# Row maxima of a streaming context attention: two of thirteen key ranges maximised as one pair, b + relu(a - b)

## Chip, cores and metric

The kernel runs on one core of one Trainium2 chip. The time is device microseconds of one execution; the profile's span runs from the first to the last instruction of one profiled execution. The engines are named as in the profile: PE is TensorE (PEld its weight loads), DVE is VectorE, ACT is ScalarE, POOL is GpSimd and SP is SyncE. They run side by side, each through its own instructions in order, and wait for each other by semaphores.

## What is computed

A decoder of two layers over 1024 tokens of width 128. Layer 0 is a Mamba block, an attention to a context of 6404 rows, and a mixture of experts; layer 1 is an attention over the tokens, a second attention to the context, and another mixture of experts. Each branch is added to its input and layer-normalised. The change is in layer 0's attention to the context, where 16 heads of width 8 share one set of keys and values:

```
c = concat([mem, kv], axis=1)             # the context rows; here only ctx_1024, 6404 of them
qh = (q @ w_q) as 16 heads of width 8
kvp = c @ w_kv
k, v = kvp[..., :8], kvp[..., 8:]
attn_prob = softmax(qh @ k.T / sqrt(8))   # 16 heads x 1024 queries x 6404 keys
out = (attn_prob @ v) as 128 columns @ w_concat
```

The softmax is taken with the row's maximum subtracted, so every query and head needs the maximum over its 6404 scores before any exponential of its row can be taken.

## The kernel before

Queries are worked through in 16 blocks. A block is 128 tokens by 8 heads, 1024 query rows. Two things are done for every block.

**Maxima.** For each of the 8 heads, 13 score tiles of 128 queries by 512 keys (the last one 260 wide) are made by PE (`max_tile`, L836) into a PSUM ring of four banks, `max_ps`. DVE takes the maximum of each tile along its keys into one column of `max_partial` (`maximum`, L1069): 104 reductions for a block. After each half of a block (`"A"` is heads 0 to 3, `"B"` heads 4 to 7) DVE reduces the columns, negates the result and splits it into a high and a low part (`negate`, L1080 to L1082), PE turns these (L843), and ACT copies them into the stacked queries (`take_shift`, L861). The maximum is thus subtracted inside the score matmul.

**Exponentials.** A block's scores come a second time, now with keys on the partitions: 51 chunks of 128 keys, each in two halves of 512 query rows, 102 steps that the code calls `e`. At step `e` PE makes the score tile (`score`, L974) into one of three banks and ACT takes its exponential into `probs` (`exponentiate`, L1053), which holds three chunks. PE multiplies the probabilities by the values (`weigh`, L963), with the sums of the probabilities in an extra column. Step `e` waits until the exponential of step `e - 3` is done. `weigh` stands behind every third step: one chunk behind steps with `e % 6 == 5`, two chunks behind steps with `e % 6 == 2`.

**The order.** While block b is exponentiated, the maxima of block b + 1 are made. A list written out in advance (`items_at`) says which maximum tile follows which score on PE: 103 tiles over the first 100 steps, about one behind each score. A maximum tile may be issued when the tile four places earlier in that list has been read (`free_place`). The two matmuls of a step stand on different halves of PE's rows. Block 0's maxima are made ahead of all exponentials, between other matmuls (queries, values, and the keys and values of layer 1).

**Keys.** They are made earlier, beside the Mamba block: `ContextKeys.make` (L365) multiplies a range of 512 context columns by the key weights, repeated over the rows; ACT adds a constant (`high_on_act`), and DVE subtracts half of the rows (`halve`, L377). The last ranges are made at the end of the Mamba block, where PE's next work is Mamba's output matmuls (L598).

## Time and profile before

| | us |
|---|---|
| median of 3 runs | 2043.5 |
| lowest and highest run | 2041.26, 2043.7 |
| profiled execution: span | 2039.6 |
| profiled execution: its own time, beside the span | not listed apart; the median is 3.9 above the span |
| PE busy | 1959.2 (96%) |
| DVE busy | 1573.2 (77%) |
| ACT busy | 1355.8 (66%) |
| POOL busy | 100.9 (5%) |

The page gives each engine's busy time and its share of the span. PE's ends are modelled and its matmuls overlap, so 96% does not say that PE is at its peak. The granted clock of PE was 0.986 of full speed over the span, and 1.00 through the whole of the attention that is changed, from 200 to 1250 us.

### The profile page before, as it was taken

To read this page: it belongs to the slowest core of one execution; us is meant where nothing else is said; L and a number is where in the kernel's file an instruction comes from. 1 tells how busy PE (TensorE), PEld (TensorE's weight loads), DVE (VectorE), ACT (ScalarE), POOL (GpSimd) and SP (SyncE) were. 2 spreads that over 40 slices of the span, in tenths; PEclk is the share of its full clock that TensorE was granted. 3 is DMA by queue.
4 is the path that set the end of the run, shared out by engine and by line. 5 is a ranking of instruction groups with operands and counts; after the bars stand their busy time and mean duration, and the time that the engine had idled before them with its cause. 6 is when DMAs were issued, how large, how long until landed. Compare 5 with 4: busy or idle time off the path is not lost. (4 is left out here: it accounts for less than half of the span.)

```text
span 2039.6 us, 36001 instructions
## 1 busy us (share of the span) xinstructions
PE 1959.2 (96%) x14245; PEld 969.3 (48%) x14245; DVE 1573.2 (77%) x2868; ACT 1355.8 (66%) x2394; POOL 100.9 (5%) x85
## 2 busy tenths in 40 slices
PE   7779999999999999999999999999999998999997
PEld 2225744444444444444444444444344444777755
DVE  7997899999999999999999981233688865444344
ACT  5333488888888888888888887432578874443321
POOL 1661000000000000000000000000200000000000
PEclk8999999999999999999999999999999999999999
DMA  4210000000000000000000000232000000000000
GB/s 148 73 62 0 1 2 2 2 1 2 1 1 2 2 1 2 2 2 1 1 2 1 2 2 1 60 120 65 0 1 1 2 1 0 1 1 1 16 29 28
DMA packets 25043, 32.66 MB, mean 16 GB/s; under 512 B 5967, under 2 KB 20335, under 8 KB 24622
## 3 DMA queue, kind: packets, MB, share of 16 engines
q1 hardware_dynamic: 23694, 28.30, 4.5%
q8 instruction: 111, 1.82, 0.4%
q10 hardware_dynamic: 1184, 2.10, 0.3%
q14 instruction: 54, 0.44, 0.1%
HBM read 29.61 MB, written 0.65 MB: 15 GB/s over the span
## 5 line engine op out<-in xcount | busy, mean ns | idle before, releaser
L1069 DVE TENSOR_REDUCE sb_max_partial<-ps_max_ps 128x1 f32<-128x512 f32 (+1 forms) x1664 | 977.3, 662 | 43.9 <-PE ps_max_ps L836 43.1
L1053 ACT ACTIVATE sb_probs<-ps_score_ps 128x512 f32<-128x512 f32 (+1 forms) x1632 | 875.1, 597 | 117.6 <-PE ps_score_ps L974 71.7
L974 PE MATMUL ps_score_ps<-sb_q_stack,sb_key_stack 64*128 64x512 f32 x1632 | 586.6, 443 | 3.9 <-ACT sb_probs L1053 3.4
L836 PE MATMUL ps_max_ps<-sb_key_stack,sb_q_stack 64*128 64x512 f32 (+1 forms) x1560 | 555.9, 438 | 0.0
L963 PE MATMUL ps_acc_ps<-sb_probs,sb_val_ones 128*32 128x256 f32 x6528 | 465.0, 387 | 0.0
L974 PEld LDWEIGHTS ps_score_ps<-sb_q_stack,sb_key_stack 64*128 64x128 f32 x1632 | 275.8, 183 | 321.5 <-ACT sb_probs L1053 257.2
L836 PEld LDWEIGHTS ps_max_ps<-sb_key_stack,sb_q_stack 64*128 64x128 f32 x1560 | 265.0, 184 | 9.8 <-DVE sb_max_partial L1069 7.5
L963 PEld LDWEIGHTS ps_acc_ps<-sb_probs,sb_val_ones 128*32 128x32 f32 x6528 | 156.3, 108 | 207.7 <-issue 140.5
L1721 DVE TENSOR_REDUCE sb_s_max_partial<-ps_s_ps 128x1 f32<-128x512 f32 x256 | 158.5, 682 | 24.6 <-PE ps_s_ps L1567 24.5
L1708 ACT ACTIVATE sb_s_probs<-ps_s_ps 128x512 f32<-128x512 f32 x256 | 140.8, 597 | 30.8 <-PE ps_s_ps L1595 22.8
L1942 DVE TENSOR_SCALAR_CACHE_REDUCE sb_x_scores<-ps_x_score_ps 128x1024 f32<-128x1024 f32 (+1 forms) x56 | 62.0, 1110 | 69.2 <-PE ps_x_score_ps L1929 69.2
L1977 ACT COPY sb_x_turned<-ps_x_turn_ps 128x512 f32<-128x512 f32 (+1 forms) x52 | 29.5, 568 | 116.8 <-PE ps_x_turn_ps L1967 116.8
L1987 PE MATMUL ps_x_acc_ps<-sb_x_turned,sb_val 128*128 128x256 f32 (+1 forms) x408 | 105.4, 381 | 0.0
L1567 PE MATMUL ps_s_ps<-sb_s_key_stack,sb_s_q_stack 64*128 64x512 f32 x256 | 103.5, 462 | 1.9 <-DVE sb_s_q_stack L1521 1.5
L1595 PE MATMUL ps_s_ps<-sb_s_q_stack,sb_s_key_stack 64*128 64x512 f32 x256 | 103.4, 464 | 0.3 <-ACT sb_s_q_stack L1699 0.2
L1929 PE MATMUL ps_x_score_ps<-sb_key_T,sb_x_q_T 128*128 128x512 f32 (+1 forms) x208 | 97.7, 579 | 1.8 <-DVE sb_x_scores L1942 1.8
L1300 DVE TENSOR_TENSOR sb_e_hidden<-sb_e_hidden,sb_e_gate_rows 128x1024 f32<-128x1024 f32 x30 | 36.7, 1226 | 75.6 <-ACT sb_e_hidden L1292 60.3
L471 PE MATMUL ps_mamba_ps<-sb_xpad,sb_ident 128*128 128x512 f32 x128 | 65.2, 632 | 23.0 <-POOL sb_xpad L536 23.0
L640 ACT ACTIVATE sb_val<-sb_delta,sb_a_neg 128x1024 f32<-128x1024 f32 x32 | 36.6, 1148 | 74.0 <-DVE sb_key_T L697 69.3
L1292 ACT ACTIVATE sb_e_hidden<-ps_e_hid_ps,sb_e_b 128x1024 f32<-128x1024 f32 x34 | 37.9, 1113 | 71.4 <-PE ps_e_hid_ps L1268 71.4
L1606 PE MATMUL ps_s_ps<-sb_s_probs,sb_s_val_ones 128*32 128x256 f32 x1024 | 81.8, 391 | 0.2 <-ACT sb_s_probs L1708 0.2
L536 POOL TENSOR_TENSOR sb_xpad<-sb_key_T,sb_val 128x1024 f32<-128x1024 f32 x31 | 73.9, 2383 | 58.3 <-DVE sb_key_T L697 57.2
(299 smaller groups left out, 1802.7 us busy)
## 6 DMA issues: line engine op xcount, KB each, us to landing
sb_val<-c_rows SPq DMA_DIRECT2D x16, 512.0 KB, 3.6
sb_e_gate_rows<-e_gate_dram SPq DMA_DIRECT2D x15, 512.0 KB, 3.9
...
```

The lines of the kernel that those rows point to most:

```text
L836: nc.tensor.matmul(bank((blk, u))[:, 0:n], queries, keys, start=True, stop=True).then_inc(tile_ready, 1)
L963: ins = nc.tensor.matmul(acc_ps[32 * q:32 * q + 32, 0:QUART], k.val_ones[:, v, :], probs[:, v % 3, q * QUART:(q + 1) * QUART], start=(v == ...
L974: nc.tensor.matmul(score_ps[:, e % 3, :], k.key_stack[rows(blk), c * P:(c + 1) * P], q_stack[rows(blk), blk // 2, j * HALF:(j + 1) * HALF] ...
L1053: nc.scalar.activation(probs[0:n, c % 3, j * HALF:(j + 1) * HALF], score_ps[0:n, e % 3, :], ACT.Exp).then_inc(exp_done, 1)
L1069: nc.vector.tensor_reduce(partial[:, blk % 2, h, r:r + 1], bank((blk, u))[:, 0:RANGES[r][1]], AX.X, ALU.max).then_inc(tile_used, 1)
L1567: nc.tensor.matmul(bank((blk, u)), q_stack[rows(blk), blk // 2, t * P:(t + 1) * P], key_stack[rows(blk), blk // 2, r * HALF:(r + 1) * HALF ...
L1595: nc.tensor.matmul(score_ps[:, n % 3, :], key_stack[rows(blk), blk // 2, c * P:(c + 1) * P], q_stack[rows(blk), blk // 2, j * HALF:(j + 1) ...
L1606: ins = nc.tensor.matmul(acc_ps[32 * q:32 * q + 32, 0:QUART], val[:, v, head(blk), :], probs[:, n % BUFS, q * QUART:(q + 1) * QUART], star ...
L1708: nc.scalar.activation(probs[:, n // 2 % BUFS, (e % 2) * HALF:(e % 2 + 1) * HALF], score_ps[:, n % 3, :], ACT.Exp).then_inc(exp_done, 1)
L1721: nc.vector.tensor_reduce(partial[:, blk % 2, t, r:r + 1], bank((blk, u)), AX.X, ALU.max).then_inc(tile_used, 1)
L1929: ins = nc.tensor.matmul(score_ps[:, at % 2, (i % 2) * HALF:(i % 2) * HALF + n], q_T[:, t * P:(t + 1) * P], k.key1_T[:, i * HALF:i * HALF ...
L1987: ins = nc.tensor.matmul(acc_ps[:, p % 2, 0:2 * P], k.val1[0:keys, c, :], turned[0:keys, G % DEPTH, 2 * j * P:2 * (j + 1) * P], start=(c = ...
```

## The change

For every head of every block, the score tile of range 7 is no longer made. In its place PE makes the tile of a difference: queries times (keys of range 7 minus keys of range 11). Call the scores of range 7 a and those of range 11 b. ACT takes relu(a - b) of that tile into an SBUF tile `raised` (`raise_tile`, L1106 of the changed kernel). When the tile of range 11 comes, DVE adds `raised` to it and takes the maximum of the sum in one call (`tensor_tensor_reduce`, L1117). As b + relu(a - b) is max(a, b), the one column stands for both ranges, and `max_partial` has 12 columns for a head in place of 13.

The difference of the keys is a 14th range of `key_stack`, made like the others: two matmuls into one bank, the first with the key weights on the columns of range 7, the second with their negative (`wk_neg`, made by POOL) on those of range 11. It is made last, after range 12. To make room in SBUF, two other tiles now share memory with older ones (`res` of the first norm with `delta`, `fin_merged` with `wk_rep`).

```
+RAISED, PLAIN_OF_PAIR = 7, 11
+DIFF_AT = NCH * P
...
-    BANK = (4, 5, 6, 7, 0, 2, 3, 0, 0, 1, 0, 1, 0)
+    BANK = (4, 5, 6, 7, 0, 2, 3, 0, 0, 1, 0, 1, 0, 1)
-    AFTER = {7: 5, 10: 9, 11: 10, 12: 11}
+    AFTER = {7: 5, 10: 9, 11: 10, 12: 11, 13: 12}
...
+        if r == self.DIFF:
+            pe.wait_ge(self.k_done, self.AFTER[r])
+            (a0, n), (b0, _) = self.RANGES[RAISED], self.RANGES[PLAIN_OF_PAIR]
+            nc.tensor.matmul(self.bank(r), k.wk_rep[:], k.ctx_T[:, a0:a0 + n], start=True, stop=False)
+            nc.tensor.matmul(self.bank(r), k.wk_neg[:], k.ctx_T[:, b0:b0 + n], start=False, stop=True).then_inc(self.k_made, 1)
+            return
...
+        for j in range(2 * 4):
+            lo = j // 4 * (P // 2) + j % 4 * HD
+            ins = nc.gpsimd.tensor_scalar(k.wk_neg[:, lo:lo + HD], w_kv[:, 0:HD], -1.0, None, ALU.mult)
...
             def max_tile(pe, blk, u):
-                h, (c0, n) = u // NR, RANGES[u % NR]
+                h, (c0, n) = u // NR, RANGES[u % NR] if u % NR != RAISED else (DIFF_AT, HALF)
...
                         nc.scalar.activation(probs[0:n, c % 3, j * HALF:(j + 1) * HALF], score_ps[0:n, e % 3, :],
                                              ACT.Exp).then_inc(exp_done, 1)
+                        for b, u in items_at[blk * NCH + c][j]:
+                            if u not in shift_ready and u % NR == RAISED:
+                                raise_tile(act, b, u)
...
+            def raise_tile(act, blk, u):
+
+                n = pair(blk, u)
+                act.wait_ge(tile_ready, blk * TILES + u + 1)
+                if n >= 2:
+                    act.wait_ge(tile_used, used((n - 2) // HB, (n - 2) % HB * NR + PLAIN_OF_PAIR))
+                nc.scalar.activation(raised[:, n % 2, :], bank((blk, u)), ACT.Relu).then_inc(raise_done, 1)
+
             def maximum(dve, blk, u):
 
                 h, r = u // NR, u % NR
+                if r == RAISED:
+                    return
                 dve.wait_ge(tile_ready, blk * TILES + u + 1)
-                nc.vector.tensor_reduce(partial[:, blk % 2, h, r:r + 1], bank((blk, u))[:, 0:RANGES[r][1]],
+                if r == PLAIN_OF_PAIR:
+                    n = pair(blk, u)
+                    dve.wait_ge(raise_done, n + 1)
+                    nc.vector.tensor_tensor_reduce(raised[:, n % 2, :], bank((blk, u)), raised[:, n % 2, :], 1.0, -3.0e38,
+                                                   ALU.add, ALU.max, partial[:, blk % 2, h, r - 1:r]).then_inc(tile_used, 1)
+                    return
+                r -= r > RAISED
+                nc.vector.tensor_reduce(partial[:, blk % 2, h, r:r + 1], bank((blk, u))[:, 0:RANGES[u % NR][1]],
                                         AX.X, ALU.max).then_inc(tile_used, 1)
```

The order of ACT's instructions in the first block, before the change. `sb_probs` is the tile of exponentials, `CAST sb_q_stack` the copy of the shift of a half block; `x58` is the number of equal instructions in a row.

```order
L1053 ACTIVATE sb_probs<-ps_score_ps 128x512 x58
L861 CAST sb_q_stack<-ps_max_ps 2x512
L1053 ACTIVATE sb_probs<-ps_score_ps 128x512 x42
L1053 ACTIVATE sb_probs<-ps_score_ps 4x512 x2
L861 CAST sb_q_stack<-ps_max_ps 2x512
```

The same place in the changed kernel, up to the fifth of the eight lifts and the shift copy behind it.

```order
L1085 ACTIVATE sb_probs<-ps_score_ps 128x512 x7
L1106 ACTIVATE sb_max_raised<-ps_max_ps 128x512
L1085 ACTIVATE sb_probs<-ps_score_ps 128x512 x13
L1106 ACTIVATE sb_max_raised<-ps_max_ps 128x512
L1085 ACTIVATE sb_probs<-ps_score_ps 128x512 x13
L1106 ACTIVATE sb_max_raised<-ps_max_ps 128x512
L1085 ACTIVATE sb_probs<-ps_score_ps 128x512 x12
L1106 ACTIVATE sb_max_raised<-ps_max_ps 128x512
L1085 ACTIVATE sb_probs<-ps_score_ps 128x512 x13
L1106 ACTIVATE sb_max_raised<-ps_max_ps 128x512
L893 CAST sb_q_stack<-ps_max_ps 2x512
```

Eight more ACTIVATE instructions now stand between the 102 exponentials of a block, behind those of steps 6, 19, 32, 44, 57, 69, 82 and 95 (counted from 0). No ACT_TABLE_LOAD stands among them.

DVE's instructions for the first half block of maxima, before the change: four heads by 13 ranges, then the three instructions of `negate`, then the second half.

```order
L1069 TENSOR_REDUCE sb_max_partial<-ps_max_ps 128x1 x52
L1080 TENSOR_REDUCE sb_neg_max<-sb_max_partial 128x4
L1081 CAST sb_neg_part<-sb_neg_max 128x4
L1082 TENSOR_TENSOR sb_neg_part<-sb_neg_max,sb_neg_part 128x4
L1069 TENSOR_REDUCE sb_max_partial<-ps_max_ps 128x1 x52
```

The same half in the changed kernel.

```order
L1121 TENSOR_REDUCE sb_max_partial<-ps_max_ps 128x1 x10
L1117 ISA sb_max_raised,sb_max_partial<-ps_max_ps,sb_max_raised 128x512
L1117 ISA sb_max_partial 128x1
L1121 TENSOR_REDUCE sb_max_partial<-ps_max_ps 128x1 x11
L1117 ISA sb_max_raised,sb_max_partial<-ps_max_ps,sb_max_raised 128x512
L1117 ISA sb_max_partial 128x1
L1121 TENSOR_REDUCE sb_max_partial<-ps_max_ps 128x1 x11
L1117 ISA sb_max_raised,sb_max_partial<-ps_max_ps,sb_max_raised 128x512
L1117 ISA sb_max_partial 128x1
L1121 TENSOR_REDUCE sb_max_partial<-ps_max_ps 128x1 x11
L1117 ISA sb_max_raised,sb_max_partial<-ps_max_ps,sb_max_raised 128x512
L1117 ISA sb_max_partial 128x1
```

Of a head's 13 reductions 11 are left, and the call on the pair is two instructions: one over the 512 elements and one that writes the 128x1 result.

PE's instructions at the end of the Mamba block, before the change. L471 adds to Mamba's running output, L365 makes a key range, L598 is the output projection.

```order
L365 MATMUL ps_mamba_ps<-sb_ctx_T,sb_wk_rep 128x512 x2
L471 MATMUL ps_mamba_ps<-sb_xpad,sb_ident 128x512 x2
L365 MATMUL ps_mamba_ps<-sb_ctx_T,sb_wk_rep 128x512
L471 MATMUL ps_mamba_ps<-sb_xpad,sb_ident 128x512 x2
L365 MATMUL ps_mamba_ps<-sb_ctx_T,sb_wk_rep 128x512
L365 MATMUL ps_mamba_ps<-sb_ctx_T,sb_wk_rep 128x260
L598 MATMUL ps_mamba_ps<-sb_w_out_T,sb_xpad 128x128 x16
```

The same place in the changed kernel.

```order
L383 MATMUL ps_mamba_ps<-sb_ctx_T,sb_wk_rep 128x512
L490 MATMUL ps_mamba_ps<-sb_xpad,sb_ident 128x512 x2
L383 MATMUL ps_mamba_ps<-sb_ctx_T,sb_wk_rep 128x512
L383 MATMUL ps_mamba_ps<-sb_ctx_T,sb_wk_rep 128x260
L372 MATMUL ps_mamba_ps<-sb_ctx_T,sb_wk_rep 128x512
L373 MATMUL ps_mamba_ps<-sb_ctx_T,sb_wk_neg 128x512
L617 MATMUL ps_mamba_ps<-sb_w_out_T,sb_xpad 128x128 x16
```

The two matmuls of the difference stand ahead of the output projection on PE, and they wait until DVE has halved range 11 (`AFTER[13]` is 12).

## Rows read from the trace of the kernel before

**Rows 1.** Page, costliest groups: count, busy us, mean ns, idle before, releaser.

```profile
L1069 DVE TENSOR_REDUCE sb_max_partial<-ps_max_ps 128x1 f32<-128x512 f32 (+1 forms) x1664 | 977.3, 662 | 43.9 <-PE ps_max_ps L836 43.1
L1053 ACT ACTIVATE sb_probs<-ps_score_ps 128x512 f32<-128x512 f32 (+1 forms) x1632 | 875.1, 597 | 117.6 <-PE ps_score_ps L974 71.7
```

**Rows 2.** Busy time of each engine from 700 to 800 us.

```profile
core 0: us, PE busy (x) PEld busy (x) DVE busy (x) ACT busy (x) POOL busy (x), PEclk, DMA share, GB/s
700.00:800.00 100.00, 99.16 (x979) 45.16 (x970) 96.65 (x175) 87.38 (x165) 0.00 (x0) 1.00 0.01 2
```

**Rows 3.** Timeline of ACT: start us, duration us, count, idle before and releaser.

```profile
716.65 3.36 ACT L1053 ACTIVATE sb_probs<-ps_score_ps 128x512 f32<-128x512 f32 x6 [0.24 <-PE ps_score_ps L974]
720.24 2.61 ACT L1053 ACTIVATE sb_probs<-ps_score_ps 128x512 f32<-128x512 f32 x5 [0.23 <-PE ps_score_ps L974]
723.01 0.60 ACT L1053 ACTIVATE sb_probs<-ps_score_ps 128x512 f32<-128x512 f32 x1 [0.16 <-PE ps_acc_ps L963]
723.84 1.58 ACT L1053 ACTIVATE sb_probs<-ps_score_ps 128x512 f32<-128x512 f32 x3 [0.23 <-PE ps_score_ps L974]
...
727.78 2.61 ACT L1053 ACTIVATE sb_probs<-ps_score_ps 128x512 f32<-128x512 f32 x5 [0.23 <-PE ps_score_ps L974]
```

**Rows 4.** Timeline of PE and its weight loads in the cycle from 716.12 us.

```profile
716.12 0.50 PE L974 MATMUL ps_score_ps<-sb_q_stack,sb_key_stack 64*128 64x512 f32 x1
...
718.28 0.18 PEld L974 LDWEIGHTS ps_score_ps<-sb_q_stack,sb_key_stack 64*128 64x128 f32 x1 [0.30 <-ACT sb_probs L1053]
...
718.71 1.07 PE L963 MATMUL ps_acc_ps<-sb_probs,sb_val_ones 128*32 128x256 f32 x16
...
719.71 0.50 PE L974 MATMUL ps_score_ps<-sb_q_stack,sb_key_stack 64*128 64x512 f32 x1
```

**Rows 5.** Waits from 320 to 1215 us: who for whom, us, times, longest.

```profile
PEld ps_score_ps L974 <- ACT sb_probs L1053: 231.3, 614, 0.6
...
PEld ps_max_ps L836 <- DVE sb_max_partial L1069: 7.0, 42, 0.2
```

**Rows 6.** Timeline of DVE: three reductions together, and one alone.

```profile
238.88 1.89 DVE L1069 TENSOR_REDUCE sb_max_partial<-ps_max_ps 128x1 f32<-128x512 f32 x3 [0.52 <-PE ps_max_ps L836]
...
254.58 0.69 DVE L1069 TENSOR_REDUCE sb_max_partial<-ps_max_ps 128x1 f32<-128x512 f32 x1 [0.86 <-PE ps_max_ps L836]
```

**Rows 7.** Timeline of DVE: two-operand instructions on PSUM, and a very short one.

```profile
144.33 2.29 DVE L697 TENSOR_TENSOR_SCAN sb_key_T<-sb_val,ps_mamba_ps 128x1024 f32<-128x1024 f32 x1
...
158.13 1.40 DVE L377 SCALAR_TENSOR_TENSOR sb_key_stack<-sb_key_stack,sb_half_sel,ps_mamba_ps 128x512 fp32r<-128x512 f32 x2
...
253.34 0.17 DVE L1081 CAST sb_neg_part<-sb_neg_max 128x4 fp32r<-128x4 f32 x1
```

**Rows 8.** Timeline: a weight load of a maximum tile that waits for DVE.

```profile
725.81 0.18 PEld L836 LDWEIGHTS ps_max_ps<-sb_key_stack,sb_q_stack 64*128 64x128 f32 x1 [0.17 <-DVE sb_max_partial L1069]
```

**Rows 9.** Timeline of ACT, later in the same block: starts of four cycles.

```profile
734.96 2.62 ACT L1053 ACTIVATE sb_probs<-ps_score_ps 128x512 f32<-128x512 f32 x5 [0.23 <-PE ps_score_ps L974]
...
738.68 0.60 ACT L1053 ACTIVATE sb_probs<-ps_score_ps 128x512 f32<-128x512 f32 x1 [0.24 <-PE ps_score_ps L974]
...
743.00 2.62 ACT L1053 ACTIVATE sb_probs<-ps_score_ps 128x512 f32<-128x512 f32 x5 [0.23 <-PE ps_score_ps L974]
...
746.94 3.35 ACT L1053 ACTIVATE sb_probs<-ps_score_ps 128x512 f32<-128x512 f32 x6 [0.23 <-PE ps_score_ps L974]
```

**Rows 10.** Timeline of PE at a block's border: the turning of shift B.

```profile
702.82 0.60 PE L843 MATMUL ps_max_ps<-sb_ident,sb_neg_part 128*2 128x128 f32 x4 [0.20 <-DVE sb_neg_part L1082]
```

**Rows 11.** Timeline of PE and DVE at the end of the Mamba block.

```profile
154.38 1.88 PE L365 MATMUL ps_mamba_ps<-sb_ctx_T,sb_wk_rep 128*128 128x512 f32 x4
...
163.74 1.14 DVE L377 SCALAR_TENSOR_TENSOR sb_key_stack<-sb_key_stack,sb_half_sel,ps_mamba_ps 128x512 fp32r<-128x512 f32 x2
163.88 3.84 PE L598 MATMUL ps_mamba_ps<-sb_w_out_T,sb_xpad 128*128 128x128 f32 x32 [0.81 <-DVE sb_xpad L706]
```

**Rows 12.** Timeline of POOL near the start.

```profile
19.53 4.26 POOL L350 TENSOR_SCALAR sb_wq_rep<-sb_x_w_q 128x64 f32<-128x64 f32 x8 [11.29 <-DMA sb_x_w_q<-L_xattn_w_q]
```

**Rows 13.** Groups from 181 to 256.8 us, block 0's maxima.

```profile
L836 PEld LDWEIGHTS ps_max_ps<-sb_key_stack,sb_q_first 128*128 128x128 f32 x104 | 18.7, 190 | 10.6 <-DVE sb_max_partial L1069 4.5 <-issue 4.3 <-ACT sb_q_stack L890 1.1
```

More of the change, by code:

```diff
@@ L190, in store, with residual_norm @@
             sp.wait_ge(self.stored, 32)
[L193 removed]
+def residual_norm(k, tag, branch, added=False, store=None, turned=None, awake=0, res=None):
     nc = k.nc
     with ExitStack() as tmp:
[L197 removed]
+        res = branch if added else res
         turned = k.ps(tag + "_turned", [P, T], tmp) if turned is None else turned
@@ L321, in load, with span @@
         eng.dma_start(self.k.ctx_T[:, cols], self.k.dram["ctx_T"][:, cols]).then_inc(self.ctx_loaded[i], 16)
+    def span(self, r):
+        return self.RANGES[r] if r < self.DIFF else (DIFF_AT, HALF)
     def bank(self, r):
-        return self.banks[:, self.BANK[r], 0:self.RANGES[r][1]]
+        return self.banks[:, self.BANK[r], 0:self.span(r)[1]]
     def columns(self, r):
-        c0, n = self.RANGES[r]
+        c0, n = self.span(r)
         return self.k.key_stack[:, c0:c0 + n]
@@ L591, in _ @@
                             keys.make(pe, keys.LATE + 2)
-                for r in range(keys.LATE + 3, len(keys.RANGES)):
+                for r in range(keys.LATE + 3, keys.COUNT):
                     keys.make(pe, r)
@@ L640, in _ @@
                         nc.scalar.activation(decay[:, s, :], delta[:, s, :], ACT.Exp, scale=a_neg[:, s, n:n + 1]).then_inc(decay_ready, 1)
-                for r in range(keys.LATE, len(keys.RANGES)):
+                for r in range(keys.LATE, keys.COUNT):
                     keys.high_on_act(act, r)
```

36 lines of the change are left out of this document (25 added, 11 removed).

## Prediction

> **What bounds the kernel now.** I read the page first, then the busy time of a stretch in the middle of the attention, then ACT's and PE's timelines over single cycles, and the waits last. The page's costliest group is the one that the change thins out: 1664 reductions on DVE, 104 for each of 16 blocks [rows 1]. From 700 to 800 us DVE is busy 96.65% and ACT 87.38% [rows 2], so DVE looks like the bound. The timelines tell another story. ACT's exponentials come in cycles of six that start 716.65, 720.24 and 723.84, so 3.59 to 3.60 us apart, and each cycle starts with a wait for a score from PE [rows 3]. Steps with e % 6 = 3, 4, 5 are the first three of a cycle, 0, 1, 2 the last three. PE's side of one cycle shows why it lasts so long [rows 4]: the first score starts at 716.12; its exponential starts at 716.65, 0.53 later; three exponentials end 2 x 0.50 + 0.60 = 1.60 later (0.50 apart, since five take 2.61 and one takes 0.60: (2.61 - 0.60) / 4 [rows 3]); at 718.28 the weights of the cycle's last score load after 0.30 of waiting for ACT, because step e needs the exponential of step e - 3; 0.43 later the double `weigh` starts, and 1.00 after that the next cycle's first score. 0.53 + 1.60 + 0.03 + 0.43 + 1.00 = 3.59. DVE is not in this ring. The waits agree: from 320 to 1215 us PE waited 231.3 us for exponentials and 7.0 us for DVE to free a maximum tile, in 42 waits, so three a block [rows 5].
>
> So I read DVE as an engine that just keeps pace. Six reductions need 6 x 0.60 = 3.60 us, 0.60 from three that take 1.89 and one that takes 0.69 [rows 6], as long as the ring, and only where a step brings a second tile, or a half block's `negate` comes between, PE has to wait.
>
> **The lifts on ACT, 8 a block, 15 blocks with maxima beside them.** A relu of 128x512 out of PSUM is not in the trace; the nearest row is the exponential of the same shape, so I take 0.50 in a busy queue. Below, nothing is the bound if ACT's waits absorb it; above, 0.60 each. What it costs depends on its step, which the order gives: 6, 19, 32, 44, 57, 69, 82, 95, so e % 6 = 0, 1, 2, 2, 3, 3, 4, 5. Behind 3 or 4 (three of them) it stands inside the three exponentials that PE's last score waits for, and the whole ring gets longer by 0.50. Behind 5, 0 or 1 (three) it delays the sixth exponential, which waited 0.16, and the next first one, which waited 0.23 [rows 3]. Six exponentials and a relu are 7 x 0.50 = 3.50, which fits into 3.59: cost nothing, with 0.09 to spare, and all of it if those waits are gone. Behind 2 (two) only the last wait is there: 723.01 + 2 x 0.50 = 724.01 against 723.84, so 0.17. A block pays 3 x 0.50 + 2 x 0.17 = 1.84, and 15 blocks 27.6 us. Behind the lift in ACT's queue stand the next exponentials, and for those PE's scores wait. PE's tile four places on waits for the lift too, but ACT is at most three steps behind PE, so it is done by then.
>
> The Trainium skill, "ScalarE: Activation LUTs", section "Rules for kernel authors", says to put relu on VectorE, which is quicker per element. Here the tiles are fp32 in PSUM, and the rows have ACT at 0.50 and DVE at 0.60 for 512 elements [rows 3, 6], so the measurement differs. At 0.60 a lift, the three in the ring would add 4.5 us to the sum.
>
> **DVE.** A head loses two reductions, 2 x 0.60, and gets the call on the pair, which is two instructions. The first reads PSUM and SBUF and writes SBUF: two `halve` of the same width take 1.40, so 0.65 to 0.70 each; the scan needs 2.29 for 1024, so 1.15 for 512 at its rate. The second writes one column; a short instruction takes 0.17 [rows 7]. The call lies between 0.60 and 1.15 + 0.17 = 1.32. It is an elementwise call with a running maximum, nearest to `halve` without its second arithmetic step: I take 0.60 + 0.15 = 0.75. DVE gets 0.45 a head lighter, 3.6 us a block. That time is not on the ring. What it buys is the waits of PE for DVE: the cycle from 723.84 to 727.78 is 3.94, 0.35 over, with a wait of 0.17 seen in it [rows 3, 8] and another like it; 734.96 to 738.68 is 3.72, 0.13 over; 743.00 to 746.94 is 3.94, 0.35 over [rows 9]. (The cycle between, 738.68 to 743.00, holds the copy of shift A and stays.) If all go, a block gains 0.83 and 15 blocks 12.5 us. The bounds are 0 and these 12.5.
>
> **Border of two blocks.** The pair of the last head is the last reduction but one before `negate`, and PE's turning of shift B waits 0.20 for DVE there [rows 10]. The call is 0.15 longer than a reduction: 15 x 0.15 = 2.3 us lost (between 0 and 15 x 0.72 = 10.8).
>
> **Keys.** The two matmuls of the difference wait for the halving of range 11, which starts at 163.74, about 0.7 before it is done, and take the 1.88 that two such matmuls take. PE's output projection, which started at 163.88, then starts near 166.3: 2.4 us on the path, for nothing else is behind it [rows 11]. ACT's and DVE's share of the 14th range lies beside the projection's 3.84. POOL's nine small instructions lie in its 11.29 of waiting [rows 12]; without that cover they would cost their own time, some 9 x 0.17 = 1.5 by the short row.
>
> **Block 0.** There PE waits 4.5 us for DVE in all [rows 13], and ACT has room. Two of 13 tiles get cheaper for DVE, PE has other matmuls between: I take 1.5 gained, of 0 to 4.5.
>
> **Sum.** 27.6 - 12.5 + 2.3 + 2.4 - 1.5 = 18.3 us. The profiled execution's span of 2039.6 becomes 2057.9; with the 3.9 by which the median of the runs lies above that span, 2061.8, say 2062.
>
> **Rivals.**
> *DVE is the bound after all.* Its 96.65% speak for it [rows 2]; if the ring's waits came from DVE, a block would be 3.6 shorter: 2043.5 - 54 + 2.4 - 1.5 = 1990. Against it: PE's 7.0 us of waiting for DVE, and that a cycle adds up to 3.59 without any DVE row. The Trainium skill, "Perfetto Trace Analysis", sections "Identifying the Most-Contended Engine" and "Optimizing Scalar/DVE Operations", holds for this rival: the engine with the highest occupancy is the one to relieve, and work of a full DVE may go to ScalarE. By its occupancy rule DVE, at 97%, would be that engine; the row of waits disagrees.
> *The lifts are absorbed.* If ACT's waits take all of them and PE's waits for DVE go, the kernel ends on the other side: 2043.5 - 12.5 + 2.3 + 2.4 - 1.5 = 2034. It needs the three lifts in the ring to cost under 0.2 each (with the sum at nothing where all lifts of a block together cost 0.62). Against it: PE's last score starts within 0.03 of the third exponential's end.
> *Half of it.* If the ring had slack that I don't see and the lifts cost half, 13.8, the sum is 4.5: 2048, within what counts as no change or just outside.
> *The pair's call is dear.* At 1.32 DVE does more than before for a head, (1.32 - 1.20) more; its waits stay, and the border loses 10.8: 2043.5 + 27.6 + 10.8 + 2.4 = 2084. It decides from 1.20 on, where two reductions cost as much.
> That the change doesn't do what it says is excluded by the order: one reduction fewer a head, and no table load between the exponentials.
>
> **Numbers.** 0.2% of the time, 4.1 us, is about what a measurement of this kernel can tell from no change. My forecast has 0.64, and its own range is 2051 (lifts in the ring at 0.40 and none behind step 2: 18 in place of 27.6) to 2073 (half the relief, and 0.35 at each border). The dear call has 0.12, the absorbed lifts 0.10, half of it 0.10 (most of it no change), DVE as the bound 0.04. Slower: 0.64 + 0.12 + 0.02 = 0.78; same 0.08; faster 0.14. The range from 2045 to 2079 leaves out the two faster rivals and the upper end of the dear call.
>
> **What would show it.** In the changed profile: cycles of 4.1 us behind steps 57, 69 and 82, of 3.75 behind 32 and 44, of 3.6 elsewhere; no cycle of 3.94 without a lift; DVE's share between 700 and 800 us falling by some 5 to 8 points, its idle time waiting for PE; blocks longer by 1.2 us (1.84 - 0.83 + 0.15); the output projection near 166. I am wrong if cycles with a lift behind steps 57, 69 or 82 stay at 3.6, if cycles without a lift get shorter than 3.59, or if the pair's two instructions take over 1.2 us together.

## The result, and the profile after

| | before | after |
|---|---|---|
| median of the runs, us | 2043.6 (4 runs, 2041.26 to 2045.17) | 2069.39 (4 runs, 2065.65 to 2069.89) |
| ratio, 95% interval | | 1.0125 [1.011, 1.0139] |
| span of the profiled execution, us | 2039.6 | 2067.7 |

The change costs 25.8 us. The forecast was 18.3 slower, 2062; the time is 7.4 above the 2062 and inside the forecast's range of 2045 to 2079.

The page of the changed kernel has ScalarE's exponentials where VectorE's reductions stood first [rows 1]. The last line is the pair's call:

```profile
L1085 ACT ACTIVATE sb_probs<-ps_score_ps 128x512 f32<-128x512 f32 (+1 forms) x1632 | 875.0, 604 | 96.1 <-PE ps_score_ps L1006 56.9
L1121 DVE TENSOR_REDUCE sb_max_partial<-ps_max_ps 128x1 f32<-128x512 f32 (+1 forms) x1408 | 846.3, 659 | 121.0 <-PE ps_max_ps L868 119.8
...
L1117 DVE CUSTOM_DVE_ANT_0 sb_max_raised<-ps_max_ps,sb_max_raised 128x512 f32<-128x512 f32 x128 | 87.6, 684 | 4.0 <-PE ps_max_ps L868 3.8
```

The reductions lost 131 us of busy time and the pair's call brought 88 of it back. VectorE's waiting for tiles grew from 43.9 to 121.0 us: the time that it was given is spent waiting, and more. The same stretch as in [rows 2], busy time from 700 to 800 us:

```profile
core 0: us, PE busy (x) PEld busy (x) DVE busy (x) ACT busy (x) POOL busy (x), PEclk, DMA share, GB/s
700.00:800.00 100.00, 98.00 (x954) 43.55 (x952) 88.34 (x167) 90.29 (x175) 0.00 (x0) 1.00 0.01 1
```

VectorE went from 96.65 to 88.34, ScalarE from 87.38 to 90.29. The waits from 330 to 1230 us (who for whom: us in all, times, longest), beside [rows 5]; L1006 is the score, L868 the maximum tile, L875 the turn of a shift, L1106 the lift:

```profile
PEld ps_score_ps L1006 <- ACT sb_probs L1085: 245.5, 660, 0.8
...
PEld ps_max_ps L868 <- ACT sb_max_raised L1106: 4.3, 14, 0.3
PEld ps_max_ps L875 <- DVE sb_max_partial L1121: 3.4, 14, 0.2
PEld ps_max_ps L868 <- DVE sb_max_partial L1121: 2.3, 14, 0.2
```

TensorE's waits for VectorE at the tiles shrank from 42 to 14, so from three a block to one, and one wait a block for a lift is new. Yet the blocks got longer. ScalarE copies the sums of a block once a block, 14 blocks between the first and the last of these rows, of before and of after:

```profile
320.94 0.37 ACT L1043 COPY sb_gathered<-ps_acc_ps 128x256 f32<-128x256 f32 x1
...
1215.86 0.37 ACT L1043 COPY sb_gathered<-ps_acc_ps 128x256 f32<-128x256 f32 x1
```

```profile
327.17 0.37 ACT L1075 COPY sb_gathered<-ps_acc_ps 128x256 f32<-128x256 f32 x1
...
1244.78 0.37 ACT L1075 COPY sb_gathered<-ps_acc_ps 128x256 f32<-128x256 f32 x1
```

(1215.86 - 320.94) / 14 = 63.92 us per block before, (1244.78 - 327.17) / 14 = 65.54 after: 1.62 more, where 1.16 was forecast. This block period is the steadiest number of a trace (the 14 single blocks lie between 63.88 and 64.00 before, between 65.50 and 65.70 after), and the experiments are read by it. ScalarE's timeline shows where in a block it arises (block 7, to be laid beside [rows 3, 9]; L1106 is a lift). Two more rows of before, then after:

```profile
731.37 2.61 ACT L1053 ACTIVATE sb_probs<-ps_score_ps 128x512 f32<-128x512 f32 x5 [0.23 <-PE ps_score_ps L974]
...
750.53 3.37 ACT L1053 ACTIVATE sb_probs<-ps_score_ps 128x512 f32<-128x512 f32 x6 [0.23 <-PE ps_score_ps L974]
```

```profile
736.37 3.36 ACT L1085 ACTIVATE sb_probs<-ps_score_ps 128x512 f32<-128x512 f32 x6 [0.23 <-PE ps_score_ps L1006]
...
740.10 1.58 ACT L1085 ACTIVATE sb_probs<-ps_score_ps 128x512 f32<-128x512 f32 x3
...
743.90 2.62 ACT L1085 ACTIVATE sb_probs<-ps_score_ps 128x512 f32<-128x512 f32 x5 [0.23 <-PE ps_score_ps L1006]
...
747.64 2.56 ACT L1085 ACTIVATE sb_probs<-ps_score_ps 128x512 f32<-128x512 f32 x5
...
751.25 3.36 ACT L1085 ACTIVATE sb_probs<-ps_score_ps 128x512 f32<-128x512 f32 x6 [0.23 <-PE ps_score_ps L1006]
754.83 0.60 ACT L1085 ACTIVATE sb_probs<-ps_score_ps 128x512 f32<-128x512 f32 x1 [0.22 <-PE ps_score_ps L1006]
755.33 0.59 ACT L1106 ACTIVATE sb_max_raised<-ps_max_ps 128x512 f32<-128x512 f32 x1
...
759.63 2.61 ACT L1085 ACTIVATE sb_probs<-ps_score_ps 128x512 f32<-128x512 f32 x5 [0.23 <-PE ps_score_ps L1006]
...
763.56 0.60 ACT L1085 ACTIVATE sb_probs<-ps_score_ps 128x512 f32<-128x512 f32 x1 [0.23 <-PE ps_score_ps L1006]
764.05 0.59 ACT L1106 ACTIVATE sb_max_raised<-ps_max_ps 128x512 f32<-128x512 f32 x1
...
767.63 1.08 ACT L1085 ACTIVATE sb_probs<-ps_score_ps 128x512 f32<-128x512 f32 x2 [0.23 <-PE ps_score_ps L1006]
```

| steps | before | after | measured | forecast |
|---|---|---|---|---|
| 27 to 33 (lift 32) | 723.84 - 720.24 = 3.60 | 740.10 - 736.37 = 3.73 | +0.13 | +0.17 |
| 33 to 39 (no lift) | 727.78 - 723.84 = 3.94 | 743.90 - 740.10 = 3.80 | -0.14 | -0.35 |
| 39 to 45 (lift 44) | 731.37 - 727.78 = 3.59 | 747.64 - 743.90 = 3.74 | +0.15 | +0.17 |
| 45 to 51 (no lift) | 734.96 - 731.37 = 3.59 | 751.25 - 747.64 = 3.61 | +0.02 | 0 |
| 51 to 57 (no lift) | 738.68 - 734.96 = 3.72 | 754.83 - 751.25 = 3.58 | -0.14 | -0.13 |
| 57 to 63 (lift 57) | 743.00 - 738.68 = 4.32 | 759.63 - 754.83 = 4.80 | +0.48 | +0.50 |
| 63 to 69 (no lift) | 746.94 - 743.00 = 3.94 | 763.56 - 759.63 = 3.93 | -0.01 | -0.35 |
| 69 to 75 (lift 69) | 750.53 - 746.94 = 3.59 | 767.63 - 763.56 = 4.07 | +0.48 | +0.50 |

"Remainder" is what is left of the step's number divided by 6, e % 6 in the prediction. The lifts behind remainder 3 (57, 69) cost what was forecast, and those behind remainder 2 (32, 44) nearly so. Of the two gains of 0.35, one did not come at all and the other is 0.14; the gain of 0.13 came.

### The profile page after: what moved, and what is told of

Read it like the earlier page. It is cut to its first block and busy times, and to the rows that moved or that the text cites. A ratio compares the mean times of both kernels' runs of the same rounds, so it can differ in the third digit from the quotient of the medians.

```text
span 2067.7 us, 36402 instructions
## 1 busy us (share of the span) xinstructions
PE 1973.6 (95%) x14249; PEld 964.3 (47%) x14249; DVE 1515.4 (73%) x2869; ACT 1406.5 (68%) x2523; POOL 102.0 (5%) x94
## 5 line engine op out<-in xcount | busy, mean ns | idle before, releaser
L1121 DVE TENSOR_REDUCE sb_max_partial<-ps_max_ps 128x1 f32<-128x512 f32 (+1 forms) x1408 | 846.3, 659 | 121.0 <-PE ps_max_ps L868 119.8
L1006 PE MATMUL ps_score_ps<-sb_q_stack,sb_key_stack 64*128 64x512 f32 x1632 | 601.4, 449 | 16.4 <-ACT sb_probs L1085 15.8
L868 PE MATMUL ps_max_ps<-sb_key_stack,sb_q_stack 64*128 64x512 f32 (+1 forms) x1560 | 568.8, 441 | 0.0
L1006 PEld LDWEIGHTS ps_score_ps<-sb_q_stack,sb_key_stack 64*128 64x128 f32 x1632 | 274.8, 184 | 356.6 <-ACT sb_probs L1085 277.5
L868 PEld LDWEIGHTS ps_max_ps<-sb_key_stack,sb_q_stack 64*128 64x128 f32 x1560 | 262.8, 184 | 8.9 <-ACT sb_max_raised L1106 4.6
L1117 DVE CUSTOM_DVE_ANT_0 sb_max_raised<-ps_max_ps,sb_max_raised 128x512 f32<-128x512 f32 x128 | 87.6, 684 | 4.0 <-PE ps_max_ps L868 3.8
```

The costliest lines, as they stand in the source:

```text
L868: nc.tensor.matmul(bank((blk, u))[:, 0:n], queries, keys, start=True, stop=True).then_inc(tile_ready, 1)
L1006: nc.tensor.matmul(score_ps[:, e % 3, :], k.key_stack[rows(blk), c * P:(c + 1) * P], q_stack[rows(blk), blk // 2, j * HALF:(j + 1) * HALF] ...
L1117: nc.vector.tensor_tensor_reduce(raised[:, n % 2, :], bank((blk, u)), raised[:, n % 2, :], 1.0, -3.0e38, ALU.add, ALU.max, partial[:, blk ...
L1121: nc.vector.tensor_reduce(partial[:, blk % 2, h, r:r + 1], bank((blk, u))[:, 0:RANGES[u % NR][1]], AX.X, ALU.max).then_inc(tile_used, 1)
```

## The experiments

The block period is (last copy of the sums - first) / 14 in each trace, as above.

| run | median, us | ratio to before [95%] | block period | VectorE, 700 to 800 us |
|---|---|---|---|---|
| before | 2041.4 to 2043.7 | 1 | 63.92 | 96.65 |
| after | 2069.39 | 1.0125 [1.011, 1.0139] | 65.54 | 88.34 |
| e1 keys only | 2045.07 | 1.0015 [1.0006, 1.0024] | 63.94 | 96.57 |
| e2 lifts only | 2128.36 | 1.0427 [1.0413, 1.0441] | 69.39 | 90.11 |
| e3 relief only | 2045.35 | 1.0012 [1.0003, 1.0021] | 63.92 | 90.16 |
| e4 free steps | 2046.99 | 1.0023 [1.0012, 1.0033] | 64.05 | 90.97 |
| e5 no double step | 2029.28 | 0.9927 [0.9914, 0.9941] | 62.95 | 91.71 |
| e6 all lifts dear | 2101.53 | 1.0281 [1.0267, 1.0295] | 67.70 | 86.26 |
| e7 early border, before | 2050.55 | 1.0037 [1.0023, 1.0051] | 64.43 | 95.38 |
| e8 early border, free steps | 2049.97 | 1.0034 [1.0022, 1.0046] | 64.19 | 89.81 |
| e9 lifts only, late | 2095.68 | 1.0254 [1.024, 1.0268] | 67.28 | 93.28 |
| e10 all behind remainder 2 | 2059.04 | 1.0069 [1.0055, 1.0082] | 64.87 | 88.81 |
| e11 score first, before | 2046.18 | 1.0015 [1.0006, 1.0024] | 64.05 | 96.26 |
| e12 score first, free steps | 2049.89 | 1.0032 [1.002, 1.0045] | 64.23 | 90.71 |

The before of each comparison ran beside it on the same chip; its medians were 2041.4 (e1 to e4), 2043.71 (e5 to e8) and 2043.16 (e9 to e12).

The same traces, cycle by cycle: from the start of one exponential in ScalarE's timeline to the start of the one six steps on, the median of 13 blocks. The first row is the length in us, the others are what the run adds to it. The head is the step that starts the cycle; the last cycle runs from step 99 over the border to step 3 of the next block.

| run | 3 | 9 | 27 | 33 | 39 | 51 | 57 | 63 | 69 | 81 | 99 |
|---|---|---|---|---|---|---|---|---|---|---|---|
| before | 3.61 | 3.59 | 3.59 | 3.94 | 3.60 | 3.71 | 4.32 | 3.94 | 3.59 | 3.60 | 4.88 |
| after | +0.08 | +0.04 | +0.14 | -0.14 | +0.14 | -0.12 | +0.48 | 0 | +0.49 | +0.48 | +0.01 |
| e3 | 0 | 0 | 0 | 0 | 0 | +0.01 | 0 | 0 | 0 | 0 | 0 |
| e4 | +0.08 | +0.04 | 0 | 0 | 0 | +0.01 | 0 | 0 | 0 | 0 | +0.01 |
| e9 | +0.08 | +0.25 | +0.21 | -0.14 | +0.46 | +0.44 | +0.49 | 0 | +0.49 | +0.48 | +0.59 |
| e10 | +0.14 | 0 | +0.14 | -0.15 | +0.14 | +0.02 | +0.01 | +0.14 | +0.01 | 0 | +0.01 |

In these runs the other cycles differ by at most 0.01, save those from 15, 75 and 87 in e10, which hold a lift and are 0.15 longer each.

**e1, the keys alone.** In the changed kernel, both `raise_tile` calls go, and `maximum` is the old one:

```diff
-                if r == RAISED:
-                    return
                 dve.wait_ge(tile_ready, blk * TILES + u + 1)
-                if r == PLAIN_OF_PAIR:
...
-                        for b, u in items_at[blk * NCH + c][j]:
-                            if u not in shift_ready and u % NR == RAISED:
-                                raise_tile(act, b, u)
```

> The 14th key range is made as in the changed kernel and the tile of differences is scored in place of the plain one, but nothing is lifted: VectorE reduces all 13 tiles of a head plainly, so the maximum of one range is left out of the shift (its difference stands in its place). Theory (the ring of TensorE and ScalarE sets the pace, VectorE does not): only the longer tail of the Mamba phase is left, +2.4 us over the kernel before, about 2046; the 3.8 us that the changed kernel loses between 30 and 160 us are a chance of its start and are not here. Rival (those 3.8 us come from the added key work on GpSimd and TensorE): 2050. The block period stays at the 63.9 us of before.

Measured: 0.15% (1.2 to 4.9 us), and the block period of before. In agreement with the 2.4 us of the longer tail. Its profiled execution does show the 3.8 us nonetheless: the last scan stands at 158.50, as in that of after.

**e2, the lifts alone.** VectorE reduces the lifted tile too, out of SBUF:

```diff
-                if r == PLAIN_OF_PAIR:
+                if r == RAISED + 1:
                     n = pair(blk, u)
                     dve.wait_ge(raise_done, n + 1)
-                    nc.vector.tensor_tensor_reduce(raised[:, n % 2, :], bank((blk, u)), raised[:, n % 2, :], 1.0, -3.0e38,
...
+                    nc.vector.tensor_reduce(partial[:, blk % 2, h, RAISED:r], raised[:, n % 2, :], AX.X, ALU.max)
```

> The lifts stay on ScalarE, but VectorE gets its 13 reductions per head back: it reduces the lifted tile plainly out of SBUF and the pair's tile plainly out of PSUM, the addition is left out. Theory (lifts cost by the step they stand at, VectorE's relief is worth little): the changed kernel plus the relief given back, 0.28 us per block as read from its trace, so about 2073; by the term on record (0.83 per block) 2082. Rival (VectorE is the bound, so the relief of 0.6 us per head is worth its whole length): 2069 + 70 = 2139. Block period 65.8 us by the theory.

Measured: 2128, far over my number, and the waits name a reason that the expectation had not counted (VectorE waiting for a lift, 330 to 1230 us):

```profile
DVE sb_max_partial L1116 <- ACT sb_max_raised L1106: 74.8, 104, 0.9
```

One position after its lift is too early: VectorE stands 0.72 us a head. So the run measured a wait on VectorE as well as its load, and it does not decide about the load. It does show that VectorE has little to spare: 8 x 0.72 = 5.8 us of standing per block, with eight more reductions, made the block 69.39 - 65.54 = 3.9 longer than in the changed kernel.

**e3, the relief alone.** VectorE skips the tile of differences, nothing is lifted, nothing waits:

```diff
                 if r == RAISED:
                     return
                 dve.wait_ge(tile_ready, blk * TILES + u + 1)
-                if r == PLAIN_OF_PAIR:
-                    n = pair(blk, u)
-                    dve.wait_ge(raise_done, n + 1)
-                    nc.vector.tensor_tensor_reduce(raised[:, n % 2, :], bank((blk, u)), raised[:, n % 2, :], 1.0, -3.0e38,
```

> VectorE skips the tile of differences altogether and reduces the pair's tile plainly, with no lift on ScalarE and no wait for one: the maximum over one range is left out of the shift. Theory: keys alone minus the relief, 4 us (0.28 per block, as the trace of the changed kernel shows) to 12 us (0.83 per block, on record): 2034 to 2042 if keys alone take 2046. Rival (VectorE is the bound): keys alone minus 70, about 1976. A second rival (no relief at all, the slips come from the steps with two maximum tiles alone): 2046.

Measured: the time of the keys alone, 63.92 per block against 63.94. Twelve reductions a head in place of thirteen are worth nothing here. VectorE's share fell from 96.57 to 90.16 and the period did not move; DVE as the bound is refuted. The Trainium skill, "Perfetto Trace Analysis", section "Identifying the Most-Contended Engine", says to work first on the engine with the highest occupancy; with TensorE's modelled matmul time left aside, that rule pointed to VectorE at 97%, and this measurement disagrees.

The profiled execution of this run is 8.6 us above its median; the surplus stands in its last block, behind the 14 that are read here.

Why did the slips stay? Not every wait did (330 to 1230 us, beside [rows 5]; L866 is the maximum tile):

```profile
PEld ps_max_ps L866 <- DVE sb_max_partial L1110: 4.6, 28, 0.2
```

Of the three waits a block of before, one is gone, that at step 33, and its cycle did not get shorter for it. Those at steps 36 and 66 are left. The cycle that holds step 33 in this run (timeline of all engines):

```profile
728.04 1.58 ACT L1083 ACTIVATE sb_probs<-ps_score_ps 128x512 f32<-128x512 f32 x3 [0.24 <-PE ps_score_ps L1004]
...
728.07 4.01 DVE L1110 TENSOR_REDUCE sb_max_partial<-ps_max_ps 128x1 f32<-128x512 f32 x7 [0.52 <-PE ps_max_ps L866]
...
730.01 0.18 PEld L866 LDWEIGHTS ps_max_ps<-sb_key_stack,sb_q_stack 64*128 64x128 f32 x1 [0.17 <-DVE sb_max_partial L1110]
...
731.97 0.60 ACT L1083 ACTIVATE sb_probs<-ps_score_ps 128x512 f32<-128x512 f32 x1 [0.23 <-PE ps_score_ps L1004]
```

The cycle is 731.97 - 728.04 = 3.93. VectorE idles 0.52 us ahead of it for want of tiles, and then has seven to reduce, 4.01 us without a pause in a cycle that otherwise takes 3.6; TensorE's tile at step 36 waits 0.17 for it, as before. The reduction saved a moment earlier became idle time: VectorE has no tile to work ahead on.

**e4, the lifts at free steps.** The whole computation; the tile of differences changes places with another tile of its head:

```diff
+    RAISED_AT = (7, 7, 6, 6, 5, 5, 8, 7)
...
+                return u % NR == RAISED_AT[u // NR]
...
+                if is_raised(u):
+                    return DIFF_AT, HALF
+                return RANGES[RAISED_AT[u // NR]] if u % NR == RAISED else RANGES[u % NR]
```

> The whole computation, with one change to the changed kernel: within a head the tile of differences stands at another position (7, 7, 6, 6, 5, 5, 8, 7 for the eight heads instead of 7), so that its lift follows the exponentials 6, 19, 31, 43, 55, 67, 83 and 95, whose remainder by 6 is 5, 0 or 1. Theory (a lift behind remainder 3 or 4 costs 0.50, behind 2 about 0.15, behind 5, 0 and 1 nothing): all of the 1.84 us per block goes, 27.6 us, so about 2042. Rival (a lift costs ScalarE's time wherever it stands, or TensorE's wait for the lift moves along with it): 2069, as the changed kernel. Half of the way, 2055, would say that the free steps are only partly free.

Measured: 2046.99, so 22.4 us of the 25.8 come back (1.49 of the 1.62 per block, which 15 times is 22.4 as well; by the ratios to the before beside each, 1.0125 and 1.0023, it is 20.8). ScalarE takes as many lifts of the same length, only elsewhere; behind one of them stand seven exponentials without a wait:

```profile
720.89 0.60 ACT L1117 ACTIVATE sb_max_raised<-ps_max_ps 128x512 f32<-128x512 f32 x1
721.37 3.97 ACT L1096 ACTIVATE sb_probs<-ps_score_ps 128x512 f32<-128x512 f32 x7
```

The lift, 0.48 to the next start, stands where ScalarE waited for TensorE in the other kernels. The rival, a lift that costs wherever it stands, falls.

One of the eight is not free. The cycles from 3 and 9 are 0.12 longer together, here and in the changed kernel, and the lift in them is the one behind step 6, the only lift behind remainder 0. From step 6 to step 15, before and in e4:

```profile
707.62 1.61 ACT L1053 ACTIVATE sb_probs<-ps_score_ps 128x512 f32<-128x512 f32 x3 [0.18 <-PE ps_score_ps L974]
...
713.05 3.37 ACT L1053 ACTIVATE sb_probs<-ps_score_ps 128x512 f32<-128x512 f32 x6 [0.23 <-PE ps_score_ps L974]
```

```profile
712.83 0.60 ACT L1096 ACTIVATE sb_probs<-ps_score_ps 128x512 f32<-128x512 f32 x1 [0.18 <-PE ps_score_ps L1017]
713.33 0.59 ACT L1117 ACTIVATE sb_max_raised<-ps_max_ps 128x512 f32<-128x512 f32 x1
...
718.39 2.61 ACT L1096 ACTIVATE sb_probs<-ps_score_ps 128x512 f32<-128x512 f32 x5 [0.23 <-PE ps_score_ps L1017]
```

713.05 - 707.62 = 5.43, and 718.39 - 712.83 = 5.56. ScalarE has just copied the sums there, so some of its waiting may be used up already; no run has a lift behind remainder 0 elsewhere, and so the place and the remainder are not parted. The other seven lifts cost at most 0.01 each.

**e5, no step with two tiles.** As e3, and the differences of heads 2, 5 and 7 are not scored:

```diff
+            GONE = (2 * NR + RAISED, 5 * NR + RAISED, 7 * NR + RAISED)
...
-                todo = list(range(1, TILES)) if b + 1 < NB else []
+                todo = [u for u in range(1, TILES) if u not in GONE] if b + 1 < NB else []
```

> As the run with VectorE's relief alone, but the differences of heads 2, 5 and 7 are not scored either: 101 maximum tiles per block in place of 104, so that no step carries two of them; the maximum over one range is left out of the shift. Question: why do the cycles behind steps 33 and 63 stay at 3.93 us with VectorE relieved? Theory now: it is TensorE's own time for the seventh tile of a cycle (0.33), no wait for VectorE. Then two cycles shrink from 3.93 to 3.60 and the tile at step 99 ends earlier: 0.66 to 1.0 us per block, 10 to 15 us, 2030 to 2035 and a block period of 62.9 to 63.3. Rival (the slip is TensorE's wait for VectorE, 0.17 once or twice a block, as the chain of waits names it): 2.5 to 5 us, 2040 to 2043.

Measured: 62.95 per block, 0.97 under e3, 0.32 for each of three tiles. So the slips come from the steps with two tiles, 33, 66 and 99. The run takes away both TensorE's own time for the seventh tile and the wait for VectorE that it brings, and so it does not part them. The wait that the trace of e3 shows at step 36 or 66 is 0.17 of a slip of 0.34; that e3 lost the wait at step 33 did not change the slip.

**e6, all lifts behind remainder 3 or 4.** As e4, with `RAISED_AT = (5, 4, 3, 9, 7, 7, 7, 6)`.

> The whole computation; the tile of differences stands in every head at a position whose lift follows an exponential of remainder 3 or 4 by 6 (steps 4, 16, 28, 46, 57, 69, 82, 94). Theory: each such lift costs its whole 0.50 us on the path, eight per block and fifteen blocks: 60 us over the run with all lifts at free steps (2047), 2107. Rival (what the free steps gained was TensorE's wait for the lift of step 32 and the like, not the remainder): 2050 to 2070.

Measured: 2101.5; (67.70 - 64.05) / 8 = 0.46 a lift. By cycles it is the 0.50 that was expected, or nearly: each of the eight that hold a lift is 0.48 or 0.49 longer than before. The mean is lower because the cycle from 51 is 0.11 shorter and the 0.12 of step 6 is not there. In the timeline of ScalarE a cycle with a lift and one without alternate:

```profile
740.41 2.61 ACT L1096 ACTIVATE sb_probs<-ps_score_ps 128x512 f32<-128x512 f32 x5 [0.23 <-PE ps_score_ps L1017]
...
744.00 1.08 ACT L1096 ACTIVATE sb_probs<-ps_score_ps 128x512 f32<-128x512 f32 x2 [0.23 <-PE ps_score_ps L1017]
744.97 0.60 ACT L1117 ACTIVATE sb_max_raised<-ps_max_ps 128x512 f32<-128x512 f32 x1
...
748.09 2.60 ACT L1096 ACTIVATE sb_probs<-ps_score_ps 128x512 f32<-128x512 f32 x5 [0.24 <-PE ps_score_ps L1017]
```

744.00 - 740.41 = 3.59, and 748.09 - 744.00 = 4.09. Same work, same lifts, 54.5 us apart from e4 by the step alone (3.65 x 15 = 54.8).

**e10, all lifts behind remainder 2.** As e4, with `RAISED_AT = (9, 8, 7, 7, 6, 6, 5, 4)`.

> The whole computation, lifts of all eight heads behind exponentials of remainder 2 by 6 (steps 8, 20, 32, 44, 56, 68, 80, 92). Theory: 0.15 us each, 1.2 per block, 18 us over the run with all lifts at free steps: 2065. Rival (a lift there is covered as well and the 0.14 of step 32 was its double step): 2047 to 2050. The other rival (0.46 each as behind remainders 3 and 4): 2102.

Measured: 2059, (64.87 - 64.05) / 8 = 0.10 a lift, two thirds of the 0.15 expected. By cycles the price is the expected one: seven of the eight that hold a lift are 0.14 or 0.15 longer. The mean is lower because the eighth (from 51) is only 0.02 longer, the cycle from 33 is 0.15 shorter, and the 0.12 of step 6 is not there. With e4 and e6 this is the price list of a lift in its own cycle: 0.49 behind remainder 3 or 4, 0.14 to 0.15 behind 2, and next to nothing behind 5 and 1; behind 0 there is only step 6, with 0.12.

**e9, the lifts alone, late.** As e2, but the lifted tile is reduced at the pair's position, right ahead of the pair's tile:

```diff
-                if r == RAISED + 1:
+                dve.wait_ge(tile_ready, blk * TILES + u + 1)
+                if r == PLAIN_OF_PAIR:
                     n = pair(blk, u)
                     dve.wait_ge(raise_done, n + 1)
-                    nc.vector.tensor_reduce(partial[:, blk % 2, h, RAISED:r], raised[:, n % 2, :], AX.X, ALU.max)
-                dve.wait_ge(tile_ready, blk * TILES + u + 1)
+                    nc.vector.tensor_reduce(partial[:, blk % 2, h, RAISED:RAISED + 1], raised[:, n % 2, :], AX.X, ALU.max)
```

> The run with lifts alone again, without the wait that it put on VectorE: the lifted tile is reduced out of SBUF only at the pair's tile, four positions after its lift. Lifts as in the changed kernel, VectorE back at 13 reductions per head, the addition left out. Theory (the relief is worth nothing, as keys alone and relief alone both show): 2069, as the changed kernel, block period 65.5. Rival (the earlier 2128 was VectorE's load and not its wait): 2120 or more.

Measured: 2095.7, so my expectation missed. VectorE no longer waits for lifts; now TensorE waits for VectorE (330 to 1230 us, to be laid beside the waits of after):

```profile
PEld ps_max_ps L875 <- DVE sb_max_partial L1118: 19.6, 27, 1.2
PEld ps_max_ps L868 <- DVE sb_max_partial L1118: 12.7, 52, 0.4
```

19.6 + 12.7 - 3.4 - 2.3 = 26.6 us over 13 to 14 blocks, against a period that is 67.28 - 65.54 = 1.74 longer. By the table of cycles 0.58 of that stands at the border, with the turn of shift B, 0.56 in the cycle from 51, ahead of the turn of shift A, and the rest in those from 9, 27 and 39. Two reductions at one position make VectorE late at these places. That is again a matter of where the work stands, not of its sum, so what the thirteenth reduction would cost in its old place, with lifts on ScalarE, was not measured.

**e7 and e8, an earlier border.** The same edit in the kernel before and in e4 (there with `RAISED_AT = (7, 6, 7, 7, 6, 6, 6, 5)`):

```diff
-            TURN_AT, LAST_AT, FIRST_TURN = 28, NCH - 1, 66
+            TURN_AT, LAST_AT, FIRST_TURN = 28, NCH - 2, 66
...
-                        if item[1] != "B":
-                            issue(pe, item)
+                        issue(pe, item)
...
-                if blk + 1 < NB:
-                    issue(pe, (blk + 1, "B"))
```

> The kernel before, with the 103 tiles of the next block spread over 98 steps in place of 100 and its second shift turned in step 101, ahead of the last three weighings, in place of behind them. In the kernel before ScalarE waits 0.95 us at each border for that turn. Theory (only the ring of TensorE and ScalarE bounds the blocks): 0.6 to 0.95 us per border, 9 to 14 us, 2027 to 2032. Rival (VectorE, 97 percent busy, can't have the maxima ready sooner, so TensorE now waits for it at the turn): no gain or a loss, 2040 to 2055.

> The changed kernel with its lifts at free steps (positions 7, 6, 7, 7, 6, 6, 6, 5) and the same earlier border: 103 tiles over 98 steps, the second shift turned in step 101. VectorE is 91 percent busy here. Theory: the border gains 0.6 to 0.95 us per block over the run with lifts at free steps (2047), 2033 to 2038. If VectorE is what holds the border in the kernel before, this kernel gains where that one does not, and the relief is worth something at last. Rival (the border is TensorE's own work, so an earlier turn only moves it): 2045 to 2050.

Measured: both slower than before. 103 tiles over 98 steps make five steps with two tiles (19, 39, 58, 78, 97) in place of three (33, 66, 99). In both runs the cycles that hold 19, 39 and 78 are 0.34 or 0.35 longer than before, and those that lost 33 and 66 as much shorter. The border's cycle is 4.69 and 4.70 in place of 4.88, so 0.18 to 0.19 shorter; e5, which has no second tile at step 99 and the old border, gained 0.26 there. So the runs show no gain by the earlier turn itself. Here VectorE's relief is worth something, 64.43 - 64.19 = 0.24 per block: the cycles from 51 and 57 are 0.25 and 0.13 longer in e7 and 0.01 each in e8, which in turn pays the 0.12 of step 6. The waits of TensorE's tiles show it (e7, then e8):

```profile
PEld ps_max_ps L836 <- DVE sb_max_partial L1066: 16.5, 83, 0.3
```

```profile
PEld ps_max_ps L879 <- DVE sb_max_partial L1129: 6.9, 42, 0.2
```

**e11 and e12, the next block's first score ahead of the turn.** In the kernel before, and in e4 with head 7's pair two positions earlier:

```diff
                 if blk + 1 < NB:
+                    score(pe, blk + 1, 0)
                     issue(pe, (blk + 1, "B"))
...
                         if e == 0 and blk > 0:
+                            take_shift(act, nc.scalar.copy, blk, "B")
                             take_acc(act, blk - 1)
```

> The kernel before with the border in another order: TensorE makes the first score of the next block ahead of the turn of the second shift, and ScalarE takes that exponential ahead of the copy of the shift, so that part of its 0.95 us of waiting is filled. Theory: 0.2 to 0.5 us per border, 3 to 7 us, 2035 to 2039. Rival (TensorE is busy through the border, so the order moves nothing): 2042.

> The changed kernel with lifts at free steps, the pair's addition of head 7 two positions earlier (9 in place of 11, out of the border), and the border's order of the run next to it. Theory: the pair's 0.1 us per border and the same 0.2 to 0.5 for the order: 4 to 9 us under 2047, 2038 to 2043, still above the kernel before in that order, because VectorE's relief pays nowhere. Rival (with VectorE relieved the border is shorter, too): 2035 or less.

Measured: no gain in either, periods of 64.05 and 64.23 against 63.92 and 64.05; the border's cycle got longer, 5.03 against 4.88 and 5.12 against 4.89. ScalarE's 0.95 of waiting at the border is not to be had by this order. No complete version tried beats the kernel before; the best with lifts is e4, 0.23% slower.

## Why the prediction was nearly right

**The ring is the bound, VectorE is not in it.** Shown by e3: one reduction in thirteen less, no change. It holds for the order that the kernel before has; with the tiles packed closer, VectorE's load counts (e7 against e8).

**Lifts, +27.6 forecast, about 27.8 measured.** The mechanism held step by step. By cycles of the changed kernel the three behind remainder 3 and 4 cost 0.48, 0.49 and 0.48 (forecast 0.50), the two behind remainder 2 0.14 each (forecast 0.17), and two of the other three nothing. The lift behind step 6 cost 0.12, which the prediction put at nothing "with 0.09 to spare". Together 1.85 per block, where 1.84 was forecast. The rivals "absorbed" and "half" fall with this; only where e4 puts the lifts are they absorbed, all but the one behind step 6.

**The step that failed is the relief of TensorE's waits for VectorE, -12.5 forecast.** The text took the cycles of 3.94 for waits that go when VectorE gets lighter. They are the steps with two maximum tiles (e5). Relief alone shortens none of the three cycles that the term counts on, from 33, 51 and 63 (e3), and with the lifts at free steps they keep their length too (e4). In the changed kernel the 3.94 behind step 63 stayed at 3.93, and "no cycle of 3.94 without a lift" was wrong. The cycles from 33 and 51 did get shorter there, by 0.14 and 0.12, so 0.26 per block and 3.9 us in place of 12.5. But they do so only in runs where a lift had made one of the two cycles ahead of them longer (32 and 44 in the changed kernel, 32 in e9 and e10, 46 in e6). So a part of those lifts is taken back; how is not shown (the lift behind step 28 in e6 left the cycle from 33 at 3.94). Net of this, moving the lifts to free steps gave 1.49 x 15 = 22.4.

**Why the number came close.** The lifts were the largest term and were right. The relief was 8.6 too large, the loss at the border 2.1 too large the other way (+2.3 forecast, 0.01 x 15 = 0.2 measured), the other terms are within 0.2: 6.6 of the 7.5 between forecast and time (25.8 - 18.3). That two of the misses partly cancel is luck. Two ends of the forecast's own range are added up a little off: its terms give 2052 in place of 2051 and 2071 in place of 2073.

**The pair's call.** 0.75 was taken for it; the timeline of VectorE shows the two instructions and the next reduction:

```profile
700.25 0.69 DVE L1117 CUSTOM_DVE_ANT_0 sb_max_raised<-ps_max_ps,sb_max_raised 128x512 f32<-128x512 f32 x1
700.87 0.08 DVE L1117 DVE_READ_ACCUMULATOR2_ANT sb_max_partial<- 128x1 f32 x1
700.87 0.42 DVE L1121 TENSOR_REDUCE sb_max_partial<-ps_max_ps 128x1 f32<-128x260 f32 x1
```

The next reduction starts 0.62 after the call, together with the short read, so the call costs a reduction and 0.02. The dear call is refuted, and so is the loss of 0.15 at the border. The 14 waits of TensorE at the turn of shift B (before, 330 to 1230 us)

```profile
PE ps_max_ps L843 <- DVE sb_neg_part L1082: 2.9, 14, 0.4
```

are none in the changed kernel, and the border's cycle is 4.89 in place of 4.88. (The 14 waits of L875 above, 0.24 each, stand at the turn of shift A, as in the kernel before.)

**Keys, +2.4 forecast.** Last scan and output projection after; the last scan of before:

```profile
158.47 2.29 DVE L716 TENSOR_TENSOR_SCAN sb_key_T<-sb_val,ps_mamba_ps 128x1024 f32<-128x1024 f32 x1
...
170.15 3.73 PE L617 MATMUL ps_mamba_ps<-sb_w_out_T,sb_xpad 128*128 128x128 f32 x32
```

```profile
154.67 2.29 DVE L697 TENSOR_TENSOR_SCAN sb_key_T<-sb_val,ps_mamba_ps 128x1024 f32<-128x1024 f32 x1
```

From scan to projection 170.15 - 158.47 = 11.68, and 163.88 - 154.67 = 9.21 before [rows 11]: +2.47. Every run with the new keys has 11.68 or 11.69, and e7 and e11, with the old ones, 9.21. e1's whole time has 3.1 (1.2 to 4.9) more.

**Block 0, -1.5 forecast.** From the projection to the first exponential the profile has 1.7 us less than before, but e1, with no relief, has 1.5 less as well, and e4, with it, only 0.2 less. The number came out, its reason was not borne out.

**Sum of the two profiled executions:** 3.8 us ahead of Mamba's last scan, 2.5 from there to the projection, 1.7 less from there to the first exponential, 1.62 x 15 = 24.3 in the blocks, and 0.8 less behind the last exponential: 28.1, the difference of the spans. Without the 3.8, which the last section treats, it is 24.3, against 25.8 by the medians.
